# Windowed attention in a six-layer network: one value projection per tile, spread to two overlapping windows by on-chip DMA

## The chip, the core and the metric

The kernel runs on one core of one Trainium2 chip. The time is device microseconds of one execution. The engines are named as in the profile: PE is TensorE (its weight loads are PEld), DVE is VectorE, ACT is ScalarE, POOL is GpSimd and SP is SyncE, which here does nothing but issue DMAs.

## The reference, cut to what matters

The program is a chain of four gated layers, each `x = x + s(xn) * silu(f(xn))`, on an input of 4 batches of 512 tokens of 128 numbers, all in fp32. The change touches one part only, the `f` of the third layer, a network of six layers that the code calls `l2_ffn_stage`. One of its layers computes, for each batch:

```
a, s = split(x); x' = concat(a, s shifted by one token)
q, k, v = split(x' @ Wqkv)              # 16 heads of 64, so 1024 numbers each
q, k = rotary(l2norm(q) * qs), rotary(l2norm(k) * ks)
out = local_attention(q, k, v)          # a query sees itself and the 32 tokens before it
x = x + out @ Wo
x = x + (a * gelu(gate) @ W2 + b2)      # a, gate from layernorm(shifted x) @ W1 + b1
```

## The kernel before, in words

The stage takes the 512 tokens of a batch as four tiles `t` of 128. Six layers of four batches make 24 iterations `it`, and 96 tiles in all. Queries are handled in blocks of 64, so a tile has two blocks, and each block needs the keys and values of its own 64 tokens and of the 32 before them: a window of `KW` = 96 rows. Windows overlap, so a token's value is needed in one window or in two. The tile `vw` holds four such windows (96 partitions of 1024 numbers), two for each of two tiles.

Work is a software pipeline written out by hand. `all_iterations` calls, for each engine, a function `slot(ahead, now, behind)` once per tile: in the same slot the attention of tile `now` is computed, the projections and rotation of the next tile `ahead` are prepared, and the feed-forward part of the tile before, `behind`, is done. Iterations 1 to 22 are a hardware loop of four slots; the first and the last iteration are written out around it. Every engine works through its own list of calls in order, and semaphores join the lists. So a slot is a repeated pattern with five orders of its own, and what sets its length is a chain that goes from engine to engine.

The order of PE in a slot is (L1550 to L1575): `mix` of behind, `turn_y` of ahead, `scores` 0, `shift`, `project` 0 (queries), `scores` 1, `turn` 0, `project` 1 (keys), `turn_xn2`, `scores` 2, `turn` 1, `pv` 0, `hidden` 1, `scores` 3, `project` 2, `turn` 2, `pv` 1, `hidden` 0, `project` 3, `turn` 3, `pv` 2, `turn_hidden`, `turn_qk` 0, `pv` 3, `feed`, `turn_qk` 1. `turn` transposes probabilities (L1469), `pv` multiplies them with `vw` (L1484), `turn_hidden` transposes the gated hidden tile `hh` (L1536), `turn_qk` transposes rotated queries and keys (L1437), `mix` is the output projection (L1494).

`project` is a helper on L1426. With k = 0 and 1 it projects the tile's 128 tokens to queries and keys. With k = 2 and 3 it projects the 96 tokens of the tile's first and second window to values. Each call is two matmuls of 512 columns in fp32, which the trace shows as four records. The values of 64 tokens in a tile are thus computed twice.

On ACT, `copy_values` (L1777) copies each of the two windows from PSUM into `vw`; it stands between `gelu` (L1831) and `copy_outputs` 2 (L1818). `copy_q` (L1785) spreads the transposed queries in four copies of 64 x 512, before `copy_outputs` 3. On DVE, the list of a slot holds the maxima (L1646), the scaling of probabilities (L1658), `copy_probs` (L1668), `normalize` (L1621), `swap` (L1630), `rotate` (L1639) and `gate_hidden` (L1704).

SP loads the weights of a layer in twelve DMAs (L1342 to L1351). Two sets are kept: those of layers 0 and 1 are loaded at once, those of layer `d` when the last tile that used their place is finished. PE waits for all twelve before the first projection of a layer.

Of the kernel before, what the change touches and what calls it, by code (L numbers as in the profile page):

```python
# [13 lines left out]
P = 128  # L14
BATCH, SEQ, D = 4, 512, 128
TILES = SEQ // P
NT = BATCH * TILES
HEADS, DH = 16, 64
PAIRS = HEADS // 2
# [1137 lines left out]
DEPTH, WINDOW, DI = 6, 32, int(D * 4 * 2 / 3)  # L1157


def l2_ffn_stage(g):  # L1160
# [14 lines left out]
    nc = g.nc  # L1175
# [14 lines left out]
    with ExitStack() as stack:  # L1190
# [19 lines left out]
        cosd = sb("cosd", [P, 2, HD])  # L1210
        qz = sb("qz", [P, PAIRS, 2, QBS, 2, QB])
        kT = sb("kT", [P, PAIRS, WINDOW + SEQ])
        vw = sb("vw", [KW, 2 * QBS, HD])
        p = sb("p", [P, 2, QUAD, KW])
        pT = sb("pT", [KW, 2, QUAD, P])
# [37 lines left out]
        q_copied = sem("q_copied")  # L1253
        k_copied = sem("k_copied")
        v_copied = sem("v_copied")

        scores_ready = sem("scores_ready")
        negmax_ready = sem("negmax_ready")
# [28 lines left out]
        def at(it, per, k):  # L1287

            return CREDIT + k + it * per

        def weight_slot(it):

# [25 lines left out]
        def banks(b0, n):  # L1318
            return g.ps[:, b0:b0 + n].rearrange("p a c -> p (a c)")
# [7 lines left out]
        @block.sync  # L1327
        def _(sp):
            start_counts(sp, sem)
            sp.dma_start(rope[:], g.c["rope"]).then_inc(const_loaded, 16)  # L1330
            sp.dma_start(band_f[:], g.c["band"]).then_inc(const_loaded, 16)
            sp.dma_start(step_down[:], g.c["step_down"]).then_inc(const_loaded, 16)
            sp.dma_start(lnp[:, 0:DEPTH], g.w["L2_ffn_ln"]).then_inc(const_loaded, 16)
            for d in range(DEPTH):
                s = d % 2
                if d >= 1:
                    sp.wait_ge(loaded, 16 * NLOAD * d)
                if d >= 2:

                    sp.wait_ge(y_ready, CREDIT + (d - 1) * BATCH * TILES)  # L1340
                for i, n in enumerate(("q_scale", "k_scale")):
                    sp.dma_start(qks[:, s, i], g.w[f"L2_ffn_{n}"][d].partition_broadcast(P)).then_inc(loaded, 16)  # L1342
                for c in range(3):
                    sp.dma_start(wqkv[:, s, c * HD:(c + 1) * HD],
                                 g.w["L2_ffn_Wqkv"][d, :, c * HD:(c + 1) * HD]).then_inc(loaded, 16)
                sp.dma_start(wo[:, s], g.w["L2_ffn_Wo"][d]).then_inc(loaded, 16)
                sp.dma_start(w1[:, s], g.w["L2_ffn_W1"][d]).then_inc(loaded, 16)
                for c, (r0, rows) in enumerate(CH):
                    sp.dma_start(w2[0:rows, s, c], g.w["L2_ffn_W2"][d, r0:r0 + rows]).then_inc(loaded, 16)
                sp.dma_start(b1[:, s], g.w["L2_ffn_b1"][d].partition_broadcast(P)).then_inc(loaded, 16)  # L1350
                sp.dma_start(b2[:, s], g.w["L2_ffn_b2"][d].partition_broadcast(P)).then_inc(loaded, 16)  # L1351

        @block.gpsimd
        def _(pool):
# [43 lines left out]
        def _(pe):  # L1398
# [8 lines left out]
            def project(it, t, k):  # L1407

                if t is None:
                    return  # L1410
                if k == 0:
                    if t == 0:
                        pe.wait_ge(loaded, (it >> LOG_BATCH) * (16 * NLOAD) + 16 * NLOAD)
                    pe.wait_ge(xs_ready, at(it, 2 * TILES, 2 * t + 2))
                    pe.wait_ge(q_copied, at(it, 2 * TILES, 2 * t))
                elif k == 1:
                    pe.wait_ge(k_copied, at(it, TILES, t))
                else:
                    pe.wait_ge(nrm_ready, at(it, 2 * TILES, 2 * t + k - 1))
                if k < 2:  # L1420
                    x, rows, c0 = xsT[:, WINDOW + t * P:WINDOW + (t + 1) * P], P, k * HD
                else:
                    w = QBS * t + k - 2
                    x, rows, c0 = xsT[:, w * QB:w * QB + KW], KW, 2 * HD
                for hf in range(2):
                    ins = nc.tensor.matmul(g.ps[0:rows, 2 * (k % 2) + hf], x,  # L1426
                                           wqkv[:, bass.ds(weight_slot(it), 1), c0 + hf * 512:c0 + (hf + 1) * 512]
                                           .rearrange("p a c -> p (a c)"), start=True, stop=True)
                ins.then_inc(projected, 1)

            def turn_qk(it, t, k):
                if t is None:
                    return
                pe.wait_ge(rotated, at(it, 2 * TILES, 2 * t + k + 1))
                pe.wait_ge(v_copied, at(it, 2 * TILES, 2 * t + k + 1))
                for c in range(PAIRS):
                    ins = nc.tensor.transpose(g.ps[:, 2 * k + c // 4, (c % 4) * P:(c % 4 + 1) * P],  # L1437
                                              cosd[:, k, c * P:(c + 1) * P], g.ident[:])
                ins.then_inc(qk_turned, 1)
# [32 lines left out]
            def pv(it, t, i):  # L1472
                if t is None:
                    return
                n = PER * t + i
                _, j, quad = step_of(n)
                if i == 0:
                    pe.wait_ge(v_copied, at(it, 2 * TILES, 2 * t + 2))
                    pe.wait_ge(y_mixed, at(it, TILES, t))
                pe.wait_ge(pT_copied, at(it, STEPS2, n + 1))  # L1480
                pe.wait_ge(oT_copied, at(it, 2 * STEPS2, 2 * n))
                for c in range(QUAD):
                    pair = quad * QUAD + c
                    ins = nc.tensor.matmul(g.ps[:, 6, c * P:(c + 1) * P],  # L1484
                                           vw[:, (QBS * t + j) % (2 * QBS), pair * P:(pair + 1) * P],
                                           pT[:, n % 2, c], start=True, stop=True)
                ins.then_inc(pv_done, 1)
# [61 lines left out]
            def slot(ahead, now, behind):  # L1549
                mix(*behind)  # L1550
                turn_y(*ahead)
                scores(*now, 0)
                shift(*behind)
                project(*ahead, 0)
                scores(*now, 1)
                turn(*now, 0)
                project(*ahead, 1)
                turn_xn2(*behind)
                scores(*now, 2)
                turn(*now, 1)  # L1560
                pv(*now, 0)
                hidden(*behind, 1)
                scores(*now, 3)
                project(*ahead, 2)
                turn(*now, 2)
                pv(*now, 1)
                hidden(*behind, 0)
                project(*ahead, 3)
                turn(*now, 3)
                pv(*now, 2)  # L1570
                turn_hidden(*behind)
                turn_qk(*ahead, 0)
                pv(*now, 3)
                feed(*behind)
                turn_qk(*ahead, 1)  # L1575
# [4 lines left out]
        def _(dve):  # L1580
            nc.vector.tensor_copy(g.gate[:], g.xn[:]).then_inc(y_started, 1)
            nc.vector.memset(xsT[:], 0.0)
            nc.vector.memset(qz[:], 0.0)
            nc.vector.memset(kT[:], 0.0).then_inc(pad_ready, 1)
            dve.wait_ge(const_loaded, 64)
# [173 lines left out]
        def _(act):  # L1759
# [8 lines left out]

            def squares(it, t, k):
                if t is not None:  # L1770
                    act.wait_ge(projected, at(it, 4 * TILES, 4 * t + k + 1))
                    nc.scalar.activation(cosd[:, k], banks(2 * k, 2), ACT.Square).then_inc(sq_ready, 1)

            def copy_values(it, t, j):
                if t is not None:
                    act.wait_ge(projected, at(it, 4 * TILES, 4 * t + j + 3))
                    nc.scalar.copy(vw[:, (QBS * t + j) % (2 * QBS)], banks(2 * j, 2)[0:KW]).then_inc(v_copied, 1)  # L1777

            def copy_q(it, t):
                if t is not None:  # L1780
                    act.wait_ge(qk_turned, at(it, 2 * TILES, 2 * t + 1))
                    for hf in range(2):
                        rows = slice(hf * DH, (hf + 1) * DH)
                        for c in range(0, PAIRS, 4):
                            ins = nc.scalar.copy(qz[rows, c:c + 4, t % 2, :, hf],  # L1785
                                                 g.ps[rows, c // 4].rearrange("p (c j q) -> p c j q", c=4, q=QB))
                        ins.then_inc(q_copied, 1)

            def copy_k(it, t):
                if t is not None:  # L1790
# [48 lines left out]
            def slot(ahead, now, behind):  # L1839
# [8 lines left out]
                exps(ch, *now, 3)  # L1848
                copy_outputs(*now, 1)
                gelu(*behind)  # L1850
                copy_values(*ahead, 0)
                copy_values(*ahead, 1)
                copy_outputs(*now, 2)
                copy_hidden(*behind)
                copy_q(*ahead)
# [634 lines left out]
```

## Time and profile before

| | |
|---|---|
| time, median of 3 runs | 5706.67 us (5686.42 to 5718.4) |
| the profiled execution | 5696.51 us |
| its span, first to last instruction | 5694.7 us |
| mean granted clock of TensorE in it | 0.889 |
| the six-layer network, first to last `turn_y` | 2042.3 to 4802.8 us |

The span is what the trace shows; the time of the same execution is 1.8 us longer. The granted clock is a share of full speed: 1.00 is 2.4 GHz and 0.50 is 1.2 GHz, the only two levels, and a figure in between is a mean over a stretch that has both. The page gives busy times of each engine; a busy share is a mean over stages with different limits, so the stage must be read by itself.

### The profile page before, as it was taken

To read this page: it belongs to the slowest core of one execution; us is meant where nothing else is said; L and a number is where in the kernel's file an instruction comes from. 1 tells how busy PE (TensorE), PEld (TensorE's weight loads), DVE (VectorE), ACT (ScalarE), POOL (GpSimd) and SP (SyncE) were. 2 spreads that over 40 slices of the span, in tenths; PEclk is the share of its full clock that TensorE was granted. 3 is DMA by queue.
4 is the path that set the end of the run, shared out by engine and by line. 5 is a ranking of instruction groups with operands and counts; after the bars stand their busy time and mean duration, and the time that the engine had idled before them with its cause. 6 is when DMAs were issued, how large, how long until landed. Compare 5 with 4: busy or idle time off the path is not lost. (4 is left out here: it accounts for less than half of the span.)

```text
span 5694.7 us, 89214 instructions
## 1 busy us (share of the span) xinstructions
PE 4468.9 (78%) x28284; PEld 3096.7 (54%) x28284; DVE 3603.6 (63%) x7261; ACT 2963.1 (52%) x8154; POOL 1958.8 (34%) x1203
## 2 busy tenths in 40 slices
PE   6887987888644458888888888888888888588788
PEld 4655665555411136666666666666666666355566
DVE  5554224455578867777777777777777777344422
ACT  3333434443233336666666666666666666233433
POOL 3433003232045444444444444444444434122300
PEclk8888999999755579999999999999999999566799
DMA  0000000000000010000000000000000000000000
GB/s 18 1 2 35 0 0 20 1 1 14 3 0 0 0 50 1 0 0 22 0 0 22 0 0 22 0 0 22 0 0 0 0 0 1 17 1 0 0 30 7
DMA packets 26280, 41.43 MB, mean 7 GB/s; under 512 B 12112, under 2 KB 18664, under 8 KB 25448
## 3 DMA queue, kind: packets, MB, share of 16 engines
q1 hardware_dynamic: 26088, 39.04, 2.0%
q8 instruction: 100, 1.64, 0.1%
q14 instruction: 92, 0.75, 0.0%
HBM read 36.93 MB, written 2.10 MB: 7 GB/s over the span
## 5 line engine op out<-in xcount | busy, mean ns | idle before, releaser
L1426 PE MATMUL ps<-l2f_wqkv,l2f_xsT 128*128 (+3 forms) x1536 | 741.4, 605 | 97.1 <-DVE xnT L1621 90.3
L1358 POOL TENSOR_TENSOR l2f_rn<-l2f_ss,neghalf 128x16 f32<-128x16 f32 x192 | 564.7, 2941 | 436.1 <-DVE l2f_ss L1615 436.1
L1803 ACT ACTIVATE l2f_p<-ps,l2f_negmax 128x96 f32<-128x96 f32 x1536 | 501.7, 338 | 282.7 <-DVE l2f_negmax L1646 279.1
L1364 POOL TENSOR_TENSOR l2f_cosd<-xnT,l2f_rot 128x1024 f32<-128x1024 f32 x192 | 487.2, 2542 | 174.8 <-DVE xnT L1621 174.8
L1484 PE MATMUL ps<-l2f_pT,l2f_vw 96*128 96x128 f32 x3072 | 423.1, 281 | 40.4 <-DVE l2f_pT L1668 40.4
L1426 PEld LDWEIGHTS ps<-l2f_wqkv,l2f_xsT 128*128 128x128 f32 (+1 forms) x1536 | 243.4, 178 | 347.8 <-issue 197.4
L1818 ACT COPY l2f_oT<-ps 64x256 f32<-64x256 f32 x768 | 281.3, 366 | 269.8 <-PE ps L1484 258.3
L1484 PEld LDWEIGHTS ps<-l2f_pT,l2f_vw 96*128 96x128 f32 x3072 | 381.7, 195 | 61.4 <-issue 56.5
L1384 POOL TENSOR_TENSOR l2f_rstd<-l2f_mv,neghalf 128x1 f32<-128x1 f32 x96 | 52.8, 550 | 1051.5 <-DVE l2f_mv L1680 1051.5
L1457 PEld LDWEIGHTS ps<-l2f_kT,l2f_qz 128*128 128x128 f32 x3072 | 399.2, 194 | 1.4 <-issue 0.3
L1457 PE MATMUL ps<-l2f_kT,l2f_qz 128*128 128x96 f32 x3072 | 398.7, 273 | 0.0
L1639 DVE TENSOR_TENSOR l2f_cosd<-l2f_cosd,xn 128x1024 f32<-128x1024 f32 x192 | 344.5, 1794 | 1.2 <-POOL l2f_cosd L1364 1.2
L1630 DVE TENSOR_TENSOR xn<-xnT,l2f_rot 128x512 f32<-128x512 f32 x384 | 332.3, 904 | 1.8 <-POOL l2f_rot L1378 1.8
L1803 ACT ACTIVATION_READ_ACCUMULATOR l2f_p<-ps,l2f_negmax 128x1 f32 x1536 | 311.3, 203 | 0.0
L1646 DVE TENSOR_REDUCE l2f_negmax<-ps 128x4 f32<-128x384 f32 x384 | 214.0, 557 | 141.3 <-PE ps L1457 130.6
L1453 PE MATMUL ps<-l2f_band,identb 128*128 128x384 bf16 x384 | 128.1, 334 | 208.3 <-ACT l2f_p L1803 201.1
L925 POOL TENSOR_TENSOR l2a_ysum<-l2a_ysum,l2a_hc 128x512 f32<-128x512 f32 x120 | 223.3, 1861 | 158.3 <-DVE l2a_hc L1081 157.2
L363 POOL TENSOR_TENSOR l1a_p<-l1a_p,l1a_rinv 128x256 f32<-128x256 f32 (+3 forms) x128 | 160.2, 1253 | 325.2 <-DVE l1a_rinv L305 325.2
L363 POOL TENSOR_TENSOR l3a_p<-l3a_p,l3a_rinv 128x64 f32<-128x64 f32 (+15 forms) x128 | 139.8, 1092 | 359.8 <-DVE l3a_rinv L305 359.8
L1668 DVE COPY l2f_pT<-ps 96x512 f32<-96x512 f32 x384 | 261.0, 680 | 0.6 <-PE ps L1469 0.6
L972 PE MATMUL ps<-l2a_split,l2a_sel 96*128 96x512 bf16 x128 | 76.9, 600 | 228.5 <-DVE l2a_hc L1081 228.5
L1658 DVE TENSOR_TENSOR l2f_p<-l2f_p,l2f_rinv 128x384 f32<-128x384 f32 x384 | 239.8, 625 | 13.2
(354 smaller groups left out, 10607.0 us busy)
## 6 DMA issues: line engine op xcount, KB each, us to landing
l2f_wqkv<-L_ffn_Wqkv_dram SPq DMA_DIRECT2D x18, 512.0 KB
l0f_w<-L_w_dram SPq DMA_DIRECT2D x2, 2304.0 KB
l3f_w<-L_w_dram SPq DMA_DIRECT2D x2, 2048.0 KB
l2f_wo<-L_ffn_Wo_dram SPq DMA_DIRECT2D x6, 512.0 KB
l2f_w<-L_ffn_W_dram SPq DMA_DIRECT2D x6, 341.0 KB
l2f_b<-L_ffn_b_dram SPq DMA_DIRECT2D x6, 341.0 KB
l1f_w<-L_w_dram SPq DMA_DIRECT2D x1, 1152.0 KB
k_turn<-l3a_kF SPq DMA_DIRECT2D x4, 256.0 KB, 2.0
```

The lines of the kernel that those rows point to most:

```text
L363: self.nc.gpsimd.tensor_tensor(self.p[:, n % 3, :, 0:nk], self.p[:, n % 3, :, 0:nk], self.rinv[:, n].unsqueeze(2).broadcast_to([P, 2, nk]) ...
L1358: nc.gpsimd.tensor_tensor(rn[:, k], ss[:, k], g.neghalf[:, 0:HEADS], ALU.pow).then_inc(rn_ready, 1)
L1364: nc.gpsimd.tensor_tensor(cosd[:, k].rearrange("p (h d) -> p h d", d=DH), nrm[:, k].rearrange("p (h d) -> p h d", d=DH), rot[:, k, 0, t].u ...
L1426: ins = nc.tensor.matmul(g.ps[0:rows, 2 * (k % 2) + hf], x, wqkv[:, bass.ds(weight_slot(it), 1), c0 + hf * 512:c0 + (hf + 1) * 512] .rearr ...
L1457: ins = nc.tensor.matmul(out[:, c * KW:(c + 1) * KW], qz[:, pair, t % 2, j].rearrange("p h q -> p (h q)"), kT[:, pair, w * QB:w * QB + KW] ...
L1484: ins = nc.tensor.matmul(g.ps[:, 6, c * P:(c + 1) * P], vw[:, (QBS * t + j) % (2 * QBS), pair * P:(pair + 1) * P], pT[:, n % 2, c], start= ...
L1630: ch.done(nc.vector.tensor_tensor(heads(swp[:, k])[:, :, to:to + 32], heads(nrm[:, k])[:, :, frm:frm + 32], rot[:, k, 1, t, to:to + 32].un ...
L1639: nc.vector.tensor_tensor(cosd[:, k], cosd[:, k], swp[:, k], ALU.add).then_inc(rotated, 1)
L1658: nc.vector.tensor_tensor(p[:, n % 2], p[:, n % 2], rinv[:, QUAD * n:QUAD * (n + 1)].unsqueeze(2).broadcast_to([P, QUAD, KW]), ALU.mult).t ...
L1668: nc.vector.tensor_copy(pT[:, n % 2].rearrange("p c q -> p (c q)"), g.ps[0:KW, 5]).then_inc(pT_copied, 1)
L1803: ins = nc.scalar.activation(p[:, n % 2, c], g.ps[:, 4, c * KW:(c + 1) * KW], ACT.Exp, bias=negmax[:, col:col + 1], accum_out=rowsum[:, co ...
L1818: nc.scalar.copy(oT[rows, quad * QUAD:(quad + 1) * QUAD, t % 2, j * QB:(j + 1) * QB], g.ps[rows, 6].rearrange("p (c h q) -> p c h q", h=2, ...
```

## The change

Values are projected once per tile, for its 128 tokens, into PSUM banks 0 and 1, and copied by ACT into a new tile `vt` with two places. `project` 3 and the second `copy_values` are gone. SP then writes the windows: a DMA of 32 rows from the tile before (not for the first tile of a batch), one of 64 rows and one of 96 rows, each row 4 KB, from `vt` to `vw`, 768 KB for a tile. Two semaphores, for even and odd tiles, count their landing. `pv` 0 waits for them, and so does the copy into `vt`, for the tiles one and two before.

SP's list changes with it: weights are no longer loaded at once. SP first waits for `band_ready`, which DVE signals after its memsets (one more is added, of 32 rows of `vw`) and the conversion of the band. Then it loads layer 0. The weights of layer 1 and later follow behind the moves of the first iteration of the layer before. Last, `copy_q` makes two copies of 64 x 1024 in place of four of 64 x 512.

```diff
+        vt = sb("vt", [P, 2, HD])
...
+        v_moved = (sem("v_moved_even"), sem("v_moved_odd"))
...
+        def moved(it, t):
+            return at(it, 80, 32 if t == 0 else 80) if t % 2 == 0 else at(it, 96, 48 * (t // 2 + 1))
...
-            for d in range(DEPTH):
+            def load_weights(d):
                 s = d % 2
                 if d >= 1:
                     sp.wait_ge(loaded, 16 * NLOAD * d)
...
+            def move_values(it, t):
+                w = QBS * (t % 2)
+                sp.wait_ge(v_copied, at(it, TILES, t + 1))
+                sp.wait_ge(pv_done, at(it, STEPS2, PER * (t - 1)))
+                if t:
+                    sp.dma_start(vw[0:WINDOW, w], vt[P - WINDOW:P, (t - 1) % 2]).then_inc(v_moved[t % 2], 16)
+                sp.dma_start(vw[WINDOW:KW, w], vt[0:QB, t % 2]).then_inc(v_moved[t % 2], 16)
+                sp.dma_start(vw[:, w + 1], vt[P - KW:P, t % 2]).then_inc(v_moved[t % 2], 16)
+
+            sp.wait_ge(band_ready, 1)
+            load_weights(0)
+            for it in range(ITERATIONS):
+                for t in range(TILES):
+                    move_values(it, t)
+                if it % BATCH == 0 and it // BATCH + 1 < DEPTH:
+                    load_weights(it // BATCH + 1)
...
-                    pe.wait_ge(nrm_ready, at(it, 2 * TILES, 2 * t + k - 1))
-                if k < 2:
-                    x, rows, c0 = xsT[:, WINDOW + t * P:WINDOW + (t + 1) * P], P, k * HD
-                else:
-                    w = QBS * t + k - 2
-                    x, rows, c0 = xsT[:, w * QB:w * QB + KW], KW, 2 * HD
+                    pe.wait_ge(nrm_ready, at(it, 2 * TILES, 2 * t + 1))
+                x, c0 = xsT[:, WINDOW + t * P:WINDOW + (t + 1) * P], k * HD
...
                 if i == 0:
-                    pe.wait_ge(v_copied, at(it, 2 * TILES, 2 * t + 2))
+                    pe.wait_ge(v_moved[t % 2], moved(it, t))
...
                 hidden(*behind, 0)
-                project(*ahead, 3)
                 turn(*now, 3)
...
+            nc.vector.memset(vw[0:WINDOW, 0], 0.0)
...
-            def copy_values(it, t, j):
+            def copy_values(it, t):
                 if t is not None:
-                    act.wait_ge(projected, at(it, 4 * TILES, 4 * t + j + 3))
-                    nc.scalar.copy(vw[:, (QBS * t + j) % (2 * QBS)], banks(2 * j, 2)[0:KW]).then_inc(v_copied, 1)
+                    act.wait_ge(projected, at(it, 3 * TILES, 3 * t + 3))
+                    for u in (t - 2, t - 1):
+                        act.wait_ge(v_moved[u % 2], moved(it, u) if u >= 0 else moved(it - 1, u + TILES))
+                    nc.scalar.copy(vt[:, t % 2], banks(0, 2)).then_inc(v_copied, 1)
...
-                        for c in range(0, PAIRS, 4):
-                            ins = nc.scalar.copy(qz[rows, c:c + 4, t % 2, :, hf],
-                                                 g.ps[rows, c // 4].rearrange("p (c j q) -> p c j q", c=4, q=QB))
-                        ins.then_inc(q_copied, 1)
+                        nc.scalar.copy(qz[rows, :, t % 2, :, hf],
+                                       banks(0, 2)[rows].rearrange("p (c j q) -> p c j q", j=QBS, q=QB)).then_inc(q_copied, 1)
...
-                copy_values(*ahead, 0)
-                copy_values(*ahead, 1)
+                copy_values(*ahead)
```

The semaphore `v_copied` now counts one per tile in place of two, and the waits of `turn_qk` on it are changed to match.

## Rows read from the trace of the kernel before

**Rows 1.** The page, its parts 1 and 2, whole span.
```profile
PE 4468.9 (78%) x28284; PEld 3096.7 (54%) x28284; DVE 3603.6 (63%) x7261; ACT 2963.1 (52%) x8154; POOL 1958.8 (34%) x1203
...
PEclk8888999999755579999999999999999999566799
```

**Rows 2.** Windows, one per loop iteration: length, busy time (instructions) by engine, clock, DMA.
```profile
2161.08:2276.67 115.59, 96.38 (x605) 70.51 (x604) 91.14 (x165) 80.10 (x228) 48.90 (x26) 1.00 0.00 1
...
2508.99:2624.57 115.58, 96.35 (x604) 70.49 (x603) 91.13 (x165) 80.11 (x228) 48.89 (x26) 1.00 0.07 27
...
3784.66:3902.87 118.21, 99.26 (x605) 73.72 (x604) 91.14 (x165) 80.09 (x228) 48.90 (x26) 0.97 0.00 0
...
sum 2556.11, PE 2136.76 PEld 1569.61 DVE 2004.12 ACT 1762.29 POOL 1075.68; mean PE 97.13 PEld 71.35 DVE 91.10 ACT 80.10 POOL 48.89
```

**Rows 3.** Windows, single slots, from one `turn_y` to the next; columns as before.
```profile
3436.89:3465.94 29.05, 24.34 (x153) 17.62 (x152) 22.99 (x41) 20.05 (x57) 14.60 (x11) 1.00 0.00 0
...
3495.63:3524.05 28.42, 23.83 (x151) 17.48 (x150) 22.69 (x42) 19.97 (x57) 11.43 (x5) 1.00 0.30 109
...
2392.25:2422.48 30.23, 25.68 (x154) 19.18 (x153) 22.99 (x41) 20.04 (x57) 14.60 (x11) 0.94 0.00 0
3844.53:3874.45 29.92, 25.33 (x151) 19.09 (x150) 22.69 (x42) 19.98 (x57) 11.42 (x5) 0.94 0.00 0
4598.80:4630.65 31.85, 27.30 (x153) 20.81 (x152) 22.99 (x41) 20.04 (x57) 14.59 (x11) 0.89 0.00 0
```

**Rows 4.** Timeline of the slot from 3495.63: start, duration, engine, line, idle before.
```profile
3504.19 1.06 PE L1484 MATMUL ps<-l2f_pT,l2f_vw 96*128 96x128 f32 x8
...
3511.61 0.74 PE L1527 MATMUL ps<-l2f_w,l2f_xnT 128*128 x2
...
3513.30 1.96 PE L1426 MATMUL ps<-l2f_wqkv,l2f_xsT 128*96 x4 [0.96 <-DVE xnT L1621]
...
3514.39 1.92 ACT L1777 COPY l2f_vw<-ps 96x1024 f32<-96x1024 f32 x2
...
3515.10 0.60 PE L1469 MATMUL ps<-ident,l2f_p 128*96 128x128 f32 x4
...
3515.54 1.06 PE L1484 MATMUL ps<-l2f_pT,l2f_vw 96*128 96x128 f32 x8
...
3517.72 0.55 PE L1536 MATMUL ps<-ident,l2f_hh 128*128 128x128 f32 x3 [1.12 <-DVE l2f_hh L1704]
...
3519.18 2.15 ACT L1785 COPY l2f_qz<-ps 64x512 f32<-64x512 f32 x4 [0.34 <-PE ps L1437]
...
3521.35 0.76 ACT L1818 COPY l2f_oT<-ps 64x256 f32<-64x256 f32 x2
...
3522.16 2.05 PE L1494 MATMUL ps<-l2f_wo,l2f_oT 128*128 x16
```

**Rows 5.** Windows: DVE's long run in that slot, and a stretch of another slot.
```profile
3508.76:3519.47 10.71, 8.30 (x45) 5.16 (x43) 10.68 (x15) 7.38 (x19) 4.97 (x2) 1.00 0.00 0
...
2414.60:2418.00 3.40, 3.32 (x16) 3.32 (x17) 2.96 (x5) 1.21 (x4) 0.00 (x0) 0.50 0.00 0
```

**Rows 6.** Timeline of PE in the slot from 2392.25, ahead of that stretch.
```profile
2409.48 1.96 PE L1426 MATMUL ps<-l2f_wqkv,l2f_xsT 128*96 x4 [0.53 <-DVE xnT L1621]
...
2414.68 0.90 PE L1536 MATMUL ps<-ident,l2f_hh 128*128 128x128 f32 x3 [1.53 <-DVE l2f_hh L1704]
```

**Rows 7.** Timeline of the stage's start.
```profile
2033.90 3.47 DVE L1583 MEMSET l2f_qz<- 128x4096 f32 x1 [0.80 <-issue]
...
2035.94 0.43 SPq L1342 DMA_DIRECT2D l2f_qks<-L_ffn_q_scale_dram  x1
...
2041.83 0.20 DVE L1586 CAST l2f_band<-l2f_band_f 128x192 bf16<-128x192 f32 x1
...
2049.53 5.30 PE L1426 MATMUL ps<-l2f_wqkv,l2f_xsT 128*128 128x512 f32 x8 [6.75 <-DMA l2f_b<-L_ffn_b_dram]
```

**Rows 8.** DMA issues: size and median time from issue to landing.
```profile
out_dram<-x SPq DMA_DIRECT2D x1, 1024.0 KB, 5.1
```

More of the change, by code:

```diff
@@ L1418, in project @@
                 else:
-                    pe.wait_ge(nrm_ready, at(it, 2 * TILES, 2 * t + k - 1))
-                if k < 2:
-                    x, rows, c0 = xsT[:, WINDOW + t * P:WINDOW + (t + 1) * P], P, k * HD
-                else:
-                    w = QBS * t + k - 2
-                    x, rows, c0 = xsT[:, w * QB:w * QB + KW], KW, 2 * HD
+                    pe.wait_ge(nrm_ready, at(it, 2 * TILES, 2 * t + 1))
+                x, c0 = xsT[:, WINDOW + t * P:WINDOW + (t + 1) * P], k * HD
                 for hf in range(2):
-                    ins = nc.tensor.matmul(g.ps[0:rows, 2 * (k % 2) + hf], x,
+                    ins = nc.tensor.matmul(g.ps[:, 2 * (k % 2) + hf], x,
                                            wqkv[:, bass.ds(weight_slot(it), 1), c0 + hf * 512:c0 + (hf + 1) * 512]
@@ L1434, in turn_qk @@
                 pe.wait_ge(rotated, at(it, 2 * TILES, 2 * t + k + 1))
-                pe.wait_ge(v_copied, at(it, 2 * TILES, 2 * t + k + 1))
+                pe.wait_ge(v_copied, at(it, TILES, t + 1))
                 for c in range(PAIRS):
@@ L1770, in squares @@
                 if t is not None:
-                    act.wait_ge(projected, at(it, 4 * TILES, 4 * t + k + 1))
+                    act.wait_ge(projected, at(it, 3 * TILES, 3 * t + k + 1))
                     nc.scalar.activation(cosd[:, k], banks(2 * k, 2), ACT.Square).then_inc(sq_ready, 1)
-            def copy_values(it, t, j):
+            def copy_values(it, t):
                 if t is not None:
-                    act.wait_ge(projected, at(it, 4 * TILES, 4 * t + j + 3))
-                    nc.scalar.copy(vw[:, (QBS * t + j) % (2 * QBS)], banks(2 * j, 2)[0:KW]).then_inc(v_copied, 1)
+                    act.wait_ge(projected, at(it, 3 * TILES, 3 * t + 3))
+                    for u in (t - 2, t - 1):
+                        act.wait_ge(v_moved[u % 2], moved(it, u) if u >= 0 else moved(it - 1, u + TILES))
+                    nc.scalar.copy(vt[:, t % 2], banks(0, 2)).then_inc(v_copied, 1)
             def copy_q(it, t):
```

## The prediction, made before the changed kernel was run

> **What bounds the kernel now.** I read the page first. PE is busy 78% of the span, more than any other engine [rows 1], which invites the thought that less PE work is less time. A share over the whole span doesn't say so for one stage; the clock line of the page adds that TensorE runs at full speed through the stage that is changed, the long row of 9s.
>
> So I cut the stage into its 22 loop iterations [rows 2]. Twelve of them take 115.57 to 115.59 us, in effect one length; the other ten take 116.57 to 118.39 us, and these are the ones whose granted clock is below 1.00. All 22 last 2556.1 us; 22 quiet ones would last 22 x 115.58 = 2542.8, so the falls of the clock cost 13.3 us. An iteration that has a layer's weights arriving beside it (27 GB/s in the DMA column) takes 115.58 us too.
>
> Within a slot the timeline tells who waits for whom [rows 4]. `project` 3 (the second L1426, 1.96 us) begins only after 0.96 us of idling for DVE's `normalize`. After it PE has `turn` 3 and `pv` 2 to do and then idles 1.12 us more, again for DVE, whose `hh` opens `turn_hidden` at 3517.72. DVE meanwhile is busy 10.68 of the 10.71 us from its last maxima to its last copy of probabilities [rows 5]. In this half of the slot DVE sets the pace and PE has slack on both sides of the matmuls that are to go. From `turn_hidden` on PE sets it: two sets of transposes, `pv` 3, `feed`, `mix`, and the next slot's scores follow with hardly a gap.
>
> **The clock.** Slots that differ only in a fall of the clock can be compared [rows 3]. A first slot of an iteration takes 29.05 us with the clock at 1.00, 30.23 with a fall in it, 31.85 with a fall twice as long. A 28.42 us slot takes 29.92 with one. So a fall costs 1.18 or 1.50 us, a long one 2.80. Where it happens is plain in one such slot: TensorE is at 0.50, that is 1.2 GHz, from 2414.60 to 2418.00 [rows 5], and that is when the PE-bound half of the slot begins. What PE did before: between the end of `project` 3 (2411.44) and `turn_hidden` (2414.68) it had 3.24 us with only 12 short records in them, and stood idle in the last 1.53 [rows 6]. In a 28.42 us slot the same thin stretch is 3517.72 - 3515.26 = 2.46 us [rows 4]. In the loop ten of 22 first slots have a fall that costs time; of 44 slots of 28.42 us one has.
>
> **The change, part by part.** *`project` 3 goes.* By itself that frees 1.96 us of PE in a place where PE waits before and after. DVE doesn't wait for it, so the direct gain is 0. But the thin stretch now begins where `hidden` 0 ends, 3511.61 + 0.74 = 3512.35, and ends where it did, since DVE's list decides that: 5.37 us in a common slot in place of 2.46, with the same 12 records inside. That is longer than the 3.24 us stretches, of which ten in 22 brought a fall. I expect a fall in nearly every slot. How long it lasts: the rows have a short kind (mean of 1.18 and 1.50: 1.34 us) and a long one (2.80 us). The stretch being about twice as long as where short ones were common, I weigh the short kind twice and the long kind once: 1.83 us, say 1.8. The bounds are 0 (no fall) and 2.8 us. There are 94 slots with all three tiles in work: 94 x 1.8 = 169 us, less the 13 us that falls cost already: +156.
>
> TensorE: Matmul & The Clock Gate in the Trainium skill says (What's actually happening) that the slow clock is the default and activity releases it, which speaks against taking matmuls out; the falls above agree, and by it the sum is the one that I make. The same page (HAM oscillation) warns of a single idle gap, longer than any that I see here before or expect after; by that alone the clock would hold. In the trace falls follow gaps of 1.53 us among sparse work, so the trace speaks against reading the warning as the only case.
>
> *One copy into `vt` in place of two into `vw`.* The two take 1.92 us on ACT and end at 3516.31; ACT's next copy needs `pv` 2, which ends at 3516.60 [rows 4]: 0.
>
> *`copy_q` in two pieces.* Its four take 2.15 us, and `copy_outputs` 3 follows it at once, and `mix` that [rows 4]. Two copies as long as those of `vw` take 1.92, 0.23 less. PE is itself only just done with `turn_qk` 1 when `mix` opens, so 0 to 0.14 us of it is gained in a slot at full clock; where the clock falls PE is mostly later than ACT. I take 0.05 x 94 = -5 us, with -13 and 0 as ends.
>
> *The moves.* Three issues of about 0.43 us each, as the weights' [rows 7], and 768 KB; the 1 MB store takes 5.1 us to land [rows 8], so 6.4 us are an upper bound. They start when the copy into `vt` ends, about 3515.4, and `pv` 0 of the next slot is due at 3504.19 + 28.42 = 3532.6: 17.2 us, nearly three times as much. Cost 0; each us beyond the cover would cost up to 94 us in all. Nothing else is hidden behind the new waits of ACT and SP in time: ACT waits for moves that were issued a slot ago; behind it stand `copy_outputs` 2 and `copy_q`, for which PE would wait. In SP's queue the weights now follow the moves and stand ahead of the next tile's, which come a slot later; the first load takes 13.6 us from issue to PE [rows 7], less than a slot, and they are needed three iterations later. That the traffic slows an engine is against the weight-carrying iteration of 115.58 us.
>
> *The start of the stage.* Weights are first issued at 2035.94 and let PE go at 2049.53 [rows 7]. They are now issued after the cast of the band, which ends at 2042.03, later by the new memset: 1024 columns at 3.47 us for 4096, 0.9 us. 2042.9 - 2035.9 = +7 us, once. PE waits for exactly this, nothing covers it. Less is possible (6), since other constants no longer share the queue.
>
> **The sum** on the profiled execution: 5694.7 + 156 - 5 + 7 = 5852.7 us of span, 1.8 more outside it: 5854.5. That execution (5696.51) lies 10 us under the median of its runs, so I name 5860, between the two bases.
>
> **Rivals.** *The clock holds.* Then the parts left are -13 to 0 and +7: 5694.7 + 1.8 - 10 + 7 = 5693.5, no change. For it: of 44 common slots only one fell before, and even if `pv` 2 moved up by all of `project` 3, PE's gap ahead of `turn_hidden` would be 1.12 + 1.96 = 3.08 us. Against it: ten falls in 22 slots after a thin stretch of 3.24 us, where 5.37 are to come. If the clock fell in half of the slots only, 94 x 0.5 x 1.8 - 13 + 2 gives 5770.
>
> *PE is what bounds, and the kernel gets faster.* If the 1.96 us come out of every slot in full, 94 x 1.96 = 184 us less: 5520. For it: PE's 78%, and 97 of 116 us of an iteration [rows 1, 2]. It decides only if DVE's run got shorter with PE's, and no wait of DVE in that run is on PE: DVE is busy in all but 0.03 us of it [rows 5].
>
> *The moves are late.* Were the pieces to land after 25 us, not 6.4, `pv` 0 would wait 8 us a slot: 94 x 8 = 752, near 6450. For it only that no row shows an on-chip DMA of this form; against it the 17 us.
>
> **How the numbers follow.** Falls in most slots: 0.80, of which half of the slots or fewer 0.05; the clock holds 0.12; PE bound 0.04; late moves 0.04. The likeliest case has its own range: 1.2 us a slot gives 94 x 1.2 - 13 + 2 = 102, so 5798; 2.4 gives 215, so 5911. I take 5800 to 5915. To leave out no more than 2 in 10 the range reaches down to the case in which the clock holds: 5690 to 5915. A difference of 0.5% (28 us) is about the least that the runs of this kernel can tell from none, as their own spread is 32 us. Faster 0.04; same 0.12, the held clock; slower 0.84, the falls and the late moves.
>
> **What would show it.** In the trace after: quiet iterations of 115.58 us gone, iterations near 115.6 + 4 x 1.8 = 122.8 us, granted clock of an iteration well under the 0.97 to 1.00 of now; between `hidden` 0 and `turn_hidden` over 5 us with 12 PE records; the clock at 0.50 when `turn_hidden` or `turn_qk` runs, its eight transposes taking nearly 2 us in place of 1.04. `turn_hidden` still waits for `hh`, DVE's run is as long as before, `pv` 0 doesn't wait for a DMA, and PE's first projection starts about 7 us later. I am wrong if the clock line still reads 1.00 in the loop, if iterations get shorter than 115.5 us, or if `pv` 0's wait ends with a DMA.

## The result, and the profile after

The changed kernel takes 5842.22 us (median of 4, 5829.66 to 5848.73) against 5705.01 (5686.42 to 5718.4) for the kernel before: 1.024 times as long, 95% interval 1.0206 to 1.0274. The profiled execution took 5829.66 us with a span of 5827.7, that is 133.0 us more than the span before. The page of it, with the three moves in its last part (size, median time from issue to landing), answers to [rows 1, 8]:

```profile
PE 4501.7 (77%) x27900; PEld 3261.2 (56%) x27900; DVE 3604.9 (62%) x7262; ACT 2865.2 (49%) x7866; POOL 1959.2 (34%) x1203
...
PEclk8888989998755578989989888988898889566799
...
l2f_vw<-l2f_vt SPq DMA_DIRECT2D x96, 384.0 KB, 4.0
l2f_vw<-l2f_vt SPq DMA_DIRECT2D x96, 256.0 KB, 3.6
...
l2f_vw<-l2f_vt SPq DMA_DIRECT2D x72, 128.0 KB, 2.3
```

PE has 384 instructions less than before and is busy 33 us longer. That can only be when the same instructions take more time, and the clock line shows why: the row of 9s of the loop is broken. The largest move lands 4.0 us after its issue in the median.

Windows of the trace after: the first iteration; the first and the last but ten of the loop; a late one; all 22 together; a second slot of an early iteration and a stretch of 3 us in it; then one slot's stretch from the end of `hidden` 0 to `turn_hidden` in two pieces. The columns are those of [rows 2].

```profile
2050.07:2178.45 128.38, 87.32 (x450) 64.88 (x451) 77.88 (x125) 59.75 (x164) 47.11 (x24) 0.79 0.20 59
2178.45:2297.90 119.45, 97.80 (x588) 76.79 (x587) 91.11 (x165) 75.93 (x216) 48.92 (x26) 0.90 0.14 41
3492.55:3612.01 119.46, 97.77 (x589) 76.80 (x588) 91.08 (x165) 75.92 (x216) 48.87 (x26) 0.90 0.14 37
...
3857.12:3980.00 122.88, 98.51 (x588) 79.23 (x587) 91.10 (x165) 76.03 (x216) 48.87 (x26) 0.89 0.10 25
...
2178.45:4840.15 2661.70, 2158.46 (x12894) 1713.76 (x12893) 2004.05 (x3630) 1671.42 (x4752) 1075.55 (x572) 0.89 0.12 30
...
2208.92:2238.49 29.57, 24.00 (x149) 17.77 (x148) 22.71 (x41) 18.87 (x54) 11.43 (x5) 0.94 0.11 28
...
2223.00:2226.00 3.00, 3.00 (x6) 1.11 (x6) 2.79 (x4) 1.40 (x8) 2.45 (x2) 0.55 0.00 0
...
2374.70:2376.98 2.28, 0.00 (x1) 0.00 (x0) 2.25 (x5) 2.23 (x4) 1.25 (x1) 0.98 0.00 0
2376.98:2380.05 3.07, 2.77 (x13) 2.48 (x13) 3.07 (x4) 1.02 (x2) 1.50 (x1) 0.50 0.37 80
```

The loop has no quiet iteration left. The first twelve take 119.46 us, one takes 122.28, the last nine 122.88: two lengths, each repeated to within 0.05 us, where before there was 115.58 and a scatter above it [rows 2]. DVE's busy time in an iteration is what it was (91.1), so DVE's list is not what got longer.

The timeline after, first the start of the stage, then PE in the slot of those two pieces; it answers to [rows 4, 6, 7]:

```profile
2039.92 0.91 DVE L1602 MEMSET l2f_vw<- 32x1024 f32 x1
...
2049.78 0.33 SPq L1348 DMA_DIRECT2D l2f_qks<-L_ffn_q_scale_dram  x1
...
2063.08 2.93 PE L1446 MATMUL ps<-l2f_wqkv,l2f_xsT 128*128 128x512 f32 x3 [12.57 <-DMA l2f_b<-L_ffn_b_dram]
...
2373.96 0.74 PE L1547 MATMUL ps<-l2f_w,l2f_xnT 128*128 x2
2377.01 1.06 PE L1489 MATMUL ps<-ident,l2f_p 128*96 128x128 f32 x4 [2.31 <-DVE l2f_pT L1688]
2377.86 1.91 PE L1504 MATMUL ps<-l2f_pT,l2f_vw 96*128 96x128 f32 x8
2380.05 0.90 PE L1556 MATMUL ps<-ident,l2f_hh 128*128 128x128 f32 x3 [0.27 <-DVE l2f_hh L1724]
2380.74 1.91 PE L1457 MATMUL ps<-ident,l2f_cosd 128*128 128x128 f32 x8
```

From 2374.70 to 2380.05, 5.35 us, PE has `turn` 3 and `pv` 2 (4 + 8 records) and stands idle 2.31 us in one piece. In the first slot of an iteration both are a little longer: 5.70 and 2.7 us. The clock goes to 0.50, that is 1.2 GHz, within the stretch, and is still there when `turn_hidden` opens the half of the slot in which PE sets the pace: the eight transposes of `turn_qk` 0 take 1.91 us.

What PE waits for in the loop: us in total, times, longest.

```profile
PE ps L1489 <- DVE l2f_pT L1688: 191.1, 88, 2.7
PE ps L1473 <- ACT l2f_p L1824: 185.0, 132, 1.7
PE ps L1556 <- DVE l2f_hh L1724: 115.8, 88, 1.5
PE ps L1504 <- DVE l2f_pT L1688: 5.5, 12, 0.5
```

These are all of them; no DMA is among them, so no `pv` is held up by a move.

### The profile page after: what moved, and what is told of

It reads as the page before. It is cut to its first block and busy times, and to the rows that moved or that the text cites. A ratio compares the mean times of both kernels' runs of the same rounds, so it can differ in the third digit from the quotient of the medians.

```text
span 5827.7 us, 88969 instructions
## 1 busy us (share of the span) xinstructions
PE 4501.7 (77%) x27900; PEld 3261.2 (56%) x27900; DVE 3604.9 (62%) x7262; ACT 2865.2 (49%) x7866; POOL 1959.2 (34%) x1203
## 5 line engine op out<-in xcount | busy, mean ns | idle before, releaser
L1446 PE MATMUL ps<-l2f_wqkv,l2f_xsT 128*128 (+1 forms) x1152 | 572.9, 622 | 17.7 <-DMA l2f_b<-L_ffn_b_dram 12.6
L1504 PE MATMUL ps<-l2f_pT,l2f_vw 96*128 96x128 f32 x3072 | 491.8, 313 | 6.5 <-DVE l2f_pT L1688 6.2
L1504 PEld LDWEIGHTS ps<-l2f_pT,l2f_vw 96*128 96x128 f32 x3072 | 456.7, 228 | 10.2 <-issue 8.3
L1489 PE MATMUL ps<-ident,l2f_p 128*96 128x128 f32 x1536 | 246.1, 285 | 208.2 <-DVE l2f_pT L1688 208.2
L1489 PEld LDWEIGHTS ps<-ident,l2f_p 128*96 128x96 f32 x1536 | 172.1, 133 | 328.2 <-DVE l2f_p L1678 257.2
L1446 PEld LDWEIGHTS ps<-l2f_wqkv,l2f_xsT 128*128 128x128 f32 x1152 | 202.3, 196 | 164.6 <-issue 145.8
L1457 PE MATMUL ps<-ident,l2f_cosd 128*128 128x128 f32 x1536 | 282.9, 346 | 8.4 <-DVE l2f_cosd L1659 8.4
```

Source lines behind the costliest of these rows:

```text
L1446: ins = nc.tensor.matmul(g.ps[:, 2 * (k % 2) + hf], x, wqkv[:, bass.ds(weight_slot(it), 1), c0 + hf * 512:c0 + (hf + 1) * 512] .rearrange( ...
L1489: ins = nc.tensor.transpose(g.ps[0:KW, 5, c * P:(c + 1) * P], p[:, n % 2, c], g.ident[:])
L1504: ins = nc.tensor.matmul(g.ps[:, 6, c * P:(c + 1) * P], vw[:, (QBS * t + j) % (2 * QBS), pair * P:(pair + 1) * P], pT[:, n % 2, c], start= ...
```

## The experiments

Every ratio is to runs of the kernel before on the same chip (medians 5704.11 us for runs 1 to 4, 5701.68 for 5 to 8, 5694.84 for 9 to 11); times from different sets are compared by these ratios or by windows. "Stretch" is the time from the end of PE's last larger piece of work (`hidden` 0 or a projection) to the start of `turn_hidden`; where nothing else is said, in a slot that isn't the first of its iteration.

**1. The matmuls back, unread.** In the changed kernel (`project` is changed to match: with k = 3 it waits for DVE's second `normalize`, as before, and signals nobody):

```diff
                 hidden(*behind, 0)
+                project(*ahead, 3)      # same input, writes PSUM banks 2 and 3, nobody reads them
                 turn(*now, 3)
```

> The changed kernel, with the two matmuls of the old project 3 put back in their old place between hidden 0 and turn 3; nothing reads what they write, and the moves, the single copy and the two-piece copy_q stay. Clock theory: the stretch between hidden 0 and turn_hidden is as it was, so the clock stays at 1.00 in the loop, iterations are 115.1 to 115.6 us long, and only the late start of the stage is left: before + 7 - (0 to 12), 5700 to 5712 us. Rival (the new waits, the moves' traffic or the other copies cost the time): the matmuls change nothing, about 5842 us, with iterations of 119 to 123 us.

Measured: 5727.47 us (5679.07 to 5738.58, 10 runs), ratio 1.0013 (0.9981 to 1.0045). An iteration, the loop, and PE ahead of `turn_hidden`:

```profile
2519.49:2634.65 115.16, 96.29 (x605) 71.35 (x604) 91.06 (x165) 76.05 (x216) 48.91 (x26) 1.00 0.13 33
2172.71:4711.50 2538.79, 2133.01 (x13247) 1582.47 (x13246) 2003.03 (x3630) 1672.93 (x4752) 1076.22 (x572) 0.99 0.12 32
```

```profile
2595.70 1.98 PE L1446 MATMUL ps<-l2f_wqkv,l2f_xsT 128*128 x4 [0.94 <-DVE xnT L1643]
...
2600.11 0.55 PE L1557 MATMUL ps<-ident,l2f_hh 128*128 128x128 f32 x3 [1.09 <-DVE l2f_hh L1726]
```

The stretch is 2600.11 - 2597.68 = 2.43 us again, the clock of the loop is 0.99, and 123 us of the loop's 2661.70 are gone, with all moves still there. The clock theory stands. The expected range of the total was missed: the ten executions form two groups, 5679 to 5695 and 5726 to 5739, one below the range and one above it. The kernel before has times of the upper kind too (5730 to 5744, in each of the three sets), so a median moves with how many of them it holds, and loops say more than totals. The execution profiled here is of the lower group; run 9 below has one of the upper kind.

**2. The kernel before without `project` 3.** Both `copy_values` copy the first window, and nothing else of the change is in it.

> The kernel before, with nothing but project 3 taken out: the second window of a tile gets the first window's values (so that part of the computation is left out); no vt, no moves, weights as early as before, copy_q in four pieces. Clock theory: falls in nearly every slot as in the changed kernel, iterations of 119 to 123 us, 5705 + 94 x 1.35 - 13 = about 5820 us, up to 5840. Rival (moves and waits cost it): 5705 us or less. Rival (PE bounds): 94 x 1.96 us less, 5520.

Measured: 5866.72 us (5852.32 to 5881.23), ratio 1.0283 (1.0232 to 1.0335).

```profile
2415.80:2538.67 122.87, 98.39 (x589) 78.81 (x588) 91.11 (x165) 79.87 (x228) 48.88 (x26) 0.89 0.00 0
...
2170.73:4862.20 2691.47, 2159.98 (x12894) 1725.60 (x12893) 2004.76 (x3630) 1757.24 (x5016) 1075.39 (x572) 0.89 0.01 5
```

Taking the two matmuls out of a slot is enough for all of the loss, and more: the time lies above the 5840 us that were the most expected. Against 22 quiet iterations of 115.58 us the loop loses 1.69 us a slot, where 1.35 had been put. No move is in this kernel, and no late start.

**3. No moves.** The changed kernel less the DMAs of `move_values` and the waits on them.

> The changed kernel without its moves between vt and vw: vw holds zeros, so the values are left out of the result; everything else, the single projection and its copy too, stays, and a larger memset costs up to 3 us once at the start. Clock theory: nothing in the loop changes, iterations of 119.5 or 122.9 us, 5835 to 5850 us. Rival (the moves' traffic, or waiting for them, makes the time): down towards 5705 to 5715 us.

Measured: 5871.15 us (5852.3 to 5882.34), ratio 1.028 (1.0229 to 1.033). The loop:

```profile
2183.28:4885.97 2702.69, 2166.72 (x12894) 1742.77 (x12893) 2004.37 (x3630) 1672.70 (x4752) 1075.57 (x572) 0.89 0.01 5
```

With 5 GB/s in place of 30 the loop is no shorter. It is longer than the changed kernel's by 41 us because it settles on 122.88 us from the start of the loop, with no stretch of 119.46; that puts the total above the expected 5835 to 5850 us. At full clock the moves cost nothing that can be seen either: an iteration takes 115.12 to 115.16 us with all of them (runs 1 and 11), 115.17 without any (run 10).

**4. Weights at once.** The changed kernel with these two lines exchanged:

```diff
-            sp.wait_ge(band_ready, 1)
             load_weights(0)
+            sp.wait_ge(band_ready, 1)
```

> The changed kernel with the first layer's weights issued as early as before, ahead of the wait for the band. Clock theory: the falls stay, only the start comes back: 5842 - 7 = 5835 us. Rival (the late start also shifts the loop into the falls): more than 20 us less.

Measured: 5844.85 us (5833.39 to 5849.83), ratio 1.023 (1.0184 to 1.0275).

```profile
2049.85:2171.35 121.50, 87.42 (x450) 64.92 (x451) 77.85 (x125) 59.75 (x164) 47.09 (x24) 0.81 0.17 50
2171.35:4867.21 2695.86, 2165.70 (x12895) 1738.86 (x12893) 2003.74 (x3630) 1672.68 (x4752) 1075.52 (x572) 0.89 0.12 30
```

The first iteration is 128.38 - 121.50 = 6.9 us shorter: the 7 us are there. The total doesn't show them, because this execution's loop settled on 122.88 us nearly throughout. A term of 7 us is below what these totals tell; the window shows it.

**5. Both.** Runs 1 and 4 together.

> The changed kernel with the two unread matmuls back between hidden 0 and turn 3, and with the first layer's weights issued ahead of the wait for the band. Clock theory: iterations of 115.15 us as with the matmuls alone, and the start comes back: about 7 us less than with the matmuls alone, 5685 to 5710 us, that is 0 to 20 us under the kernel before. Rival (the late start is no cost, something else in the loop is): no difference to the matmuls alone.

Measured: 5686.34 us (5674.0 to 5722.41, 12 runs), ratio 0.9969 (0.9942 to 0.9997). Its first iteration takes 117.40 us, against 124.33 in run 1.

**6. `project` 2 in the place.** No unread work: the changed kernel's own value projection goes where `project` 3 was.

```diff
-                project(*ahead, 2)
                 turn(*now, 2)
                 pv(*now, 1)
                 hidden(*behind, 0)
+                project(*ahead, 2)
                 turn(*now, 3)
```

> The changed kernel with its only other candidate for the place, project 2, moved from ahead of turn 2 to the old place of project 3, behind hidden 0; it starts there as soon as hidden 0 ends. PE has the same work as in the changed kernel. It would end some 4.5 us ahead of turn_hidden, where the two unread matmuls ended 2.5 us ahead. Clock theory, by the length of the thin stretch: 4.5 us are nearer to the 5.35 us of the changed kernel than to 2.46, so most slots still fall, 5780 to 5845 us. Rival (the amount of PE's work in that half of the slot decides, not where it lies): 5700 to 5720 us.

Measured: 5855.21 us (5848.87 to 5881.03), ratio 1.0266 (1.0214 to 1.0317).

```profile
2525.01 1.88 PE L1446 MATMUL ps<-l2f_wqkv,l2f_xsT 128*128 x4
2529.22 0.61 PE L1489 MATMUL ps<-ident,l2f_p 128*96 128x128 f32 x4 [2.33 <-DVE l2f_pT L1688]
...
2532.25 0.90 PE L1556 MATMUL ps<-ident,l2f_hh 128*128 128x128 f32 x3 [1.53 <-DVE l2f_hh L1724]
```

The expected 4.5 us were wrong: with `project` 2 out of its old place everything ahead of it moved up by as much, and it ends at 2526.89, 5.36 us ahead of `turn_hidden`, as far as `hidden` 0 in the changed kernel. So the time is near that of the changed kernel, above the expected 5780 to 5845 us. What counts is when the work lies, and an order in a list doesn't fix that where the engine has slack.

**7. One matmul back.** Run 1 with one of the two.

> The changed kernel with only one of the two unread matmuls back (0.98 us in place of 1.96). Clock theory, by the length of the thin stretch: it becomes about 3.4 us, near the 3.24 us of the kernel before after which ten first slots in 22 had a fall; so a part of the slots fall, about half: 5705 + 47 x 1.35 + 7 - 10 = 5765 us, between 5720 and 5830. If any matmul in the place is enough: about 5712. If it takes both: about 5842.

Measured: 5792.43 us (5747.25 to 5805.47), ratio 1.0127 (1.007 to 1.0185). The stretch is 3283.37 - 3280.09 = 3.28 us, near the expected 3.4; in first slots it is 4.07.

```profile
3278.97 1.12 PE L1446 MATMUL ps<-l2f_wqkv,l2f_xsT 128*128 x2 [0.98 <-DVE xnT L1643]
...
3283.37 0.55 PE L1557 MATMUL ps<-ident,l2f_hh 128*128 128x128 f32 x3 [1.53 <-DVE l2f_hh L1726]
```

Iterations of both kinds alternate:

```profile
3231.16:3346.28 115.12, 93.35 (x596) 69.58 (x595) 91.12 (x165) 75.96 (x216) 48.87 (x26) 1.00 0.11 26
3582.55:3701.95 119.40, 98.05 (x597) 74.36 (x595) 91.12 (x165) 75.97 (x216) 48.87 (x26) 0.96 0.14 41
2170.02:4770.57 2600.55, 2129.83 (x13070) 1610.09 (x13069) 2003.43 (x3630) 1671.00 (x4752) 1075.18 (x572) 0.97 0.12 31
```

The total holds more than the loop: behind the last `turn_y` this execution takes 930.8 us, the kernel before 891.9, as in the upper execution of run 9.

**8. `project` 2 in the place, and late.** Run 6 with one number changed: in `project`, k = 2 waits for `nrm_ready` 2t + 2 in place of 2t + 1, DVE's second `normalize`.

> As the run with project 2 moved, but project 2 waits there for DVE's second normalize, as the old project 3 did; so it runs some 2 us later and ends about 2.5 us ahead of turn_hidden. Not one instruction more or less than in the changed kernel. Clock theory, by the length of the thin stretch: 2.5 us as in the kernel before, the clock holds unless the stretch ahead of project 2, now with 1.9 us less work, falls in its place: 5695 to 5720 us, with iterations of 115.1 to 115.6 us. Rival (PE's total work in the slot decides): about 5842 us, as the changed kernel.

Measured: 5720.33 us (5708.55 to 5750.3, 10 runs), ratio 1.0029 (1.0 to 1.0058).

```profile
3081.92 0.74 PE L1547 MATMUL ps<-l2f_w,l2f_xnT 128*128 x2
3085.34 1.98 PE L1446 MATMUL ps<-l2f_wqkv,l2f_xsT 128*128 x4 [2.68 <-DVE xnT L1641]
...
3089.74 0.55 PE L1556 MATMUL ps<-ident,l2f_hh 128*128 128x128 f32 x3 [1.09 <-DVE l2f_hh L1724]
```

```profile
2980.48:3095.97 115.49, 94.42 (x589) 71.66 (x587) 90.06 (x165) 75.56 (x216) 48.84 (x26) 0.96 0.12 29
...
2166.50:4728.11 2561.61, 2076.73 (x12894) 1569.50 (x12893) 2000.67 (x3630) 1658.25 (x4752) 1074.48 (x572) 0.95 0.12 32
```

This is the sharpest of the runs: the instructions of run 6, made to wait longer, and 131 us less of loop. The amount of PE's work is not what decides. The clock still falls: in this iteration three times, at 0.50 for over 3 us from 2998.6, 3022.5 and 3056.7 on. But all three falls are over ahead of `turn_hidden`, while DVE sets the pace, and an iteration with a clock of 0.96 takes 115.49 us, next to nothing more than 115.15. The whole loop says the same: its clock is 0.95, below the 0.97 of run 7, and yet it is 39 us shorter.

**9. Run 8 with the weights at once.**

> The run in which project 2 waits in the old place of project 3, and with the first layer's weights issued ahead of the wait for the band. It has no unread matmul. Clock theory: 7 us less than without the early weights, 5705 to 5720 us, equal to the kernel before within what can be measured. Rival (the early weights give nothing): about 5720 us or more.

Measured: 5709.76 us (5699.55 to 5754.01, 10 runs), ratio 1.0033 (1.001 to 1.0056). The ratio is that of run 8 (1.0029), so no gain shows in the total, on run 8 or on the kernel before. The start did come back: counted from the stage's first copy on DVE, the first projection comes after 18.5 us, in run 8 after 24.8. But the first iteration is only 3.0 us shorter (119.77 against 122.78), since falls take more of it; its second slot takes 32.05 us against 28.62. The profiled execution is one of the upper group: span 5752.1 against 5715.8 in run 8. The loops are alike (2563.88 and 2561.61); behind the last `turn_y` it takes 933.1 us in place of 900.5, with clocks of 0.54 to 0.64 in the 500 us after 4950 where run 8 has 0.62 to 0.70. So here the upper group came from what follows the loop, which the change doesn't touch; that this holds for the upper times of runs 1 and 5 too was not seen.

**10. `copy_q` alone.** The kernel before with `copy_q` in two pieces.

> The kernel before with copy_q in two pieces and nothing else changed. By the iterations of 115.15 us in the run with the matmuls back, against 115.58: 0.43 us an iteration, or 0.11 a slot, 94 x 0.11 = 10 us less, about 5695 us, with quiet iterations of 115.1 to 115.2 us. If those 0.43 us came from the single copy of the values: 115.58 and no change.

Measured: 5683.63 us (5675.14 to 5693.47, 10 runs), ratio 0.9971 (0.9951 to 0.9991).

```profile
2398.27:2513.44 115.17, 96.03 (x605) 70.47 (x604) 91.16 (x165) 79.72 (x220) 48.92 (x26) 1.00 0.00 0
```

115.58 - 115.17 = 0.41 us an iteration, 0.10 a slot, 9 us in the loop, and the whole kernel is 0.3% faster: the one part of the change that pays. (Its loop of 2538.3 us is 17.8 shorter than before; the other 9 are fewer falls that cost.)

**11. A third matmul.** Run 5 with one more unread matmul of 512 columns between `pv` 2 and `turn_hidden`.

> The run with both unread matmuls back and the weights early, and a third unread matmul (0.98 us) between pv 2 and turn_hidden, where PE idles 1.12 us for DVE. Clock theory: the stretch ahead of turn_hidden is filled to the end, so the last falls in the loop go and the first slots stay at 28.95 us; PE isn't late, since it idled there: 5675 to 5690 us, up to 20 us under the kernel before. Rival (PE's work bounds there): up to 94 x 0.98 us more, 5780.

Measured: 5673.4 us (5664.06 to 5710.79, 12 runs), ratio 0.9962 (0.9938 to 0.9985), 0.4% under the kernel before. Run 10 has 0.9971, so the totals don't tell what of this is the third matmul's; the loop does.

```profile
2498.64 1.02 PE L1446 MATMUL ps<-l2f_wqkv,l2f_xsT 128*128 x2
2499.90 0.55 PE L1557 MATMUL ps<-ident,l2f_hh 128*128 128x128 f32 x3 [0.24 <-DVE l2f_hh L1727]
```

```profile
2391.00:2506.12 115.12, 99.72 (x612) 72.23 (x611) 91.09 (x165) 75.95 (x216) 48.88 (x26) 1.00 0.11 26
2160.73:4693.91 2533.18, 2195.41 (x13422) 1590.53 (x13421) 2003.96 (x3630) 1671.10 (x4752) 1075.53 (x572) 1.00 0.12 32
```

One fall is left in the loop, and the iteration that has it takes 115.29 us: 22 iterations in 2533.18 us are 115.14 each, with PE busier than in any other run. So 2533.2 us is, to 0.2 us, the loop with two-piece `copy_q` and no falls, and the others can be set against it (in brackets the stretch of first slots, where it differs):

| kernel | stretch, us | loop of 22, us | over 2533.2, per slot (of 88) |
|---|---|---|---|
| third matmul (11) | 0.24 (0.67) | 2533.18 | 0 |
| both matmuls back (1) | 2.43 (3.22) | 2538.79 | 0.06 |
| `project` 2 late (8) | 2.42 in the slot shown, after a gap of 2.68 | 2561.61 | 0.32 |
| one matmul back (7) | 3.28 (4.07) | 2600.55 | 0.77 |
| changed kernel | 5.35 (5.70) | 2661.70 | 1.46 |
| `project` 2 early (6) | 5.36 | 2692.76 | 1.81 |

Among the kernels that differ only in how much lies in the place (11, 1, 7 and the changed one) the loss grows with the stretch. It isn't set by the stretch alone: run 8 loses five times what run 1 does at the same 2.4 us, with falls ahead of `project` 2 and during it. Nor does a length decide each time. First slots have 3.24 us in the kernel before and 3.22 in run 1, and in nine of 22 there, in three of 22 here, a fall costs a microsecond or more. What decides between two such slots stays open.

## Why the prediction was right, step by step

**The bound.** Right: DVE sets the pace up to `hh`, PE from there on. `turn_hidden` waits for `hh` as before, and DVE's busy time is unchanged. No part of the removed 1.96 us came out of the slot; the rival in which PE bounds (5520 us) is refuted by run 2, where only those matmuls go.

**The falls.** The mechanism was right, and so was the length of the stretch, 5.37 us forecast and 5.35 found. (The count of falls before was off by one: thirteen of 22 iterations were quiet, not twelve, and nine first slots had a fall that cost time, not ten. The 13.3 us don't change by it.) The price needs two readings. Each of the two iteration lengths gives one: (119.46 - 115.14) / 4 = 1.08 us a slot in the first twelve iterations, (122.88 - 115.14) / 4 = 1.94 in the last nine; 1.46 over the loop, against 1.8 forecast. Runs 3, 4 and 6, which settled almost wholly on 122.88, have 1.93, 1.85 and 1.81. So 1.8 fits the commoner of the two rhythms, and the profiled execution spent half of its loop in the cheaper one. In that one, one of an iteration's four falls is free: in the second slot the clock is down between 2223 and 2227, ahead of `hidden` 0, where DVE sets the pace, and the slot takes 29.57 us, as at full clock (29.58 in run 1). The other three cost 1.2 to 1.6 us, against 1.6 to 2.2 for the four of a 122.88 us iteration (30.81, 31.19, 30.36 and 30.52 us against 28.95, 29.58, 28.30 and 28.32 in run 1). The prediction weighed only how long a fall lasts; where in the slot it lies was the missing half of the price.

So the 1.8 was met in part by luck. It was made of two short falls and a long one, and [rows 3] tell the kinds by a slot's clock: 0.94 and 0.89. The lines show first slots of both lengths of iteration after, the slot of run 1 with which the free one was compared, and the long fall of the kernel before:

```profile
2178.45:2208.92 30.47, 24.43 (x149) 19.64 (x148) 22.99 (x41) 19.04 (x54) 14.61 (x11) 0.89 0.24 79
...
3857.12:3887.93 30.81, 24.79 (x150) 19.98 (x149) 22.99 (x41) 19.04 (x54) 14.59 (x11) 0.89 0.09 21
...
2548.45:2578.03 29.58, 24.14 (x154) 17.92 (x152) 22.68 (x41) 18.98 (x54) 11.43 (x5) 1.00 0.11 27
...
4622.90:4629.80 6.90, 6.69 (x31) 6.70 (x32) 2.02 (x5) 3.66 (x7) 0.00 (x0) 0.51 0.00 0
```

Every slot of a 122.88 us iteration, and three of four in the other kind, have the long fall, which the prediction gave one slot in three. But none costs 2.80 us. The long fall before came 1.7 us behind the start of its `turn_hidden` (4621.24); those after begin ahead of theirs, and the earlier they begin the less they cost: 2.2 us where it is 0.7 us ahead, 1.2 where it is 3.2 (the slot of 2374.70 above). There were more long falls than forecast and each was cheaper, and the two errors met near 1.8.

The Trainium skill, TensorE: Matmul & The Clock Gate (What's actually happening), has it that the slow clock is the default and activity lifts it. The runs agree in the plainest way: two unread matmuls take the kernel from 1.024 to 1.001 times the time before. The same page's section HAM oscillation warns of one long idle gap; by that alone the clock would hold in all of these kernels. The measurement decides: with no gap in the loop above 2.7 us the changed kernel's clock falls in every slot. Run 8 has gaps as long as that (2.68 us above) and is better by 100 us of loop, with a projection behind the gap. So here the length of one gap is not what tells the kernels apart.

**`copy_q`.** -5 us forecast, -13 to 0 as bounds; 22 x 0.41 = 9 us in the loop (run 10). The two copies take 2.04 us, not the 1.92 of those of `vw`, yet the gain is most of the 0.14 that was the limit. The trace of the changed kernel:

```profile
2353.11 2.04 ACT L1807 COPY l2f_qz<-ps 64x1024 f32<-64x1024 f32 x2 [0.34 <-PE ps L1457]
```

**The copy into `vt` and the moves.** 0 forecast; run 3 without moves is not faster, an iteration at full clock is as long with them as without, and PE's waits name no DMA. The late-moves rival falls: 4.0 us at most in the medians, under the bound of 6.4.

**The start.** +7 us forecast. The first projection is at 2063.08, 13.55 later than before; 6.66 of it were there ahead of the stage's first copy (2037.96 against 2031.30), which leaves 6.89. Runs 4 and 5 give back 6.9 us each.

**The sum.** +158 us forecast; +133.0 found in the profiled execution (5860 us named, 5842.22 the median): 6.7 ahead of the stage, 6.9 at its start, 3.8 more in the first iteration, 105.6 in the loop, 4.2 in the last three slots and 5.8 behind them. The loop's 105.6 are falls of 128.5, less 13.3 that were paid before, less 9.6 by which 22 quiet iterations became shorter (9 of it for `copy_q`, by run 10): 2533.2 + 128.5 = 2661.7. The first and the last of the six are scatter of stages that the change leaves alone: behind the last `turn_y` the kernel before takes 891.9 us, the changed kernel 897.7, run 3 890.9. That the clock might hold had a chance of 0.12; it holds only where the place is filled.

## What to carry to other kernels

Work on an engine with slack isn't free to remove when that engine's clock depends on what it did last: find what PE does just before the stretch in which it sets the pace, and keep that dense. Where work is saved, ask whether what is left can be made to lie there; one wait on a later event (run 8) won back most of what the saving had lost. And price a fall of the clock by where it lies, not only by how long it is.

## What the runs showed of the hardware that was not expected

The falls lock to the loop. In the changed kernel the iterations take 119.46 or 122.88 us and repeat that nine times and more in a row, to within 0.05 us. Kernels with the same loop settle differently: the changed kernel went from one to the other after twelve iterations, run 4 took 122.88 from the third on for the most part, 34 us more of loop. Run 7 goes through a pattern of about six iterations (121.2, 119.4, 119.4, 119.8, 115.1, 115.1) and begins again. So 34 to 41 us of such a kernel's total (runs 4 and 3) may be the choice of rhythm and nothing else, and a single length of iteration says more than the total. Why a kernel settles on one of them was not tested. And a DMA from one place of on-chip memory to another, of 128 to 384 KB, landed 2.3 to 4.0 us after its issue, with no cost to any engine that the trace shows.
